# Extra products and a later place for the gates' products in the opening, silu's table loaded one phase earlier

## What is computed

```
mod = (silu(L0_c) @ L0_wmod).reshape(2, 6, 1, -1)
sa, ca, ga, sb, cb, gb = mod[:, 0], ..., mod[:, 5]
ga = (2 * (ga >= 0) - 1) * maximum(abs(ga), 0.25)
h = layernorm(x) * (1 + ca) + sa
q, k, v = h @ Wq.T, h @ Wk.T, h @ Wv.T          # rope on q and k, elu + 1
state = state + k_s v_s^T;  z = z + k_s          # over the sequence
out = (q_s @ state) / (q_s . z + 1e-6)
x = x + ga * (out @ Wo.T)
h = layernorm(x) * (1 + cb) + sb
x = x + gb * (sparsify_2to4(silu(h @ w_gate) * (h @ w_up)) @ w_down)
```

## Time and profile before

| what | value |
|---|---|
| median of 3 runs | 1020.46 us (1020.2 to 1021.85) |
| the profiled execution's own time | 1021.04 us |
| its span (first to last instruction) | 1019.1 us |
| mean granted clock of TensorE | 0.993 |
| busy: TensorE, weight loads, VectorE, ScalarE, POOL | 96%, 78%, 66%, 33%, 25% |
| opening, until TensorE's first transpose of a feature (L744) | 0 to 32.7 us |
| attention | until 538.4 us |

### The profile page before, as it was taken

One profiled execution on the slowest core, in us unless ns is written; L12 is line 12 of the kernel. 1 busy time (PEld: TensorE's weight loads), 2 busy tenths in 40 slices (PEclk: granted clock), 3 DMA queues, 4 the chain that ended last, 5 costly groups with the idle time before them and its releaser, 6 DMA issues. The chain is left out here.

```text
span 1019.1 us, 15660 instructions
## 1 busy us (share of the span) xinstructions
PE 978.2 (96%) x5978; PEld 790.9 (78%) x5978; DVE 676.8 (66%) x1488; ACT 334.1 (33%) x606; POOL 254.6 (25%) x322
## 2 busy tenths in 40 slices
PE   6899999999999999999999999998999999999997
PEld 5688888888888888888877888886666667778875
DVE  6666766667666676666666977774667776476556
ACT  4333334333344333343333331221132233322220
POOL 2222212222123231222221000024244554211111
PEclk9799999999999999999999999999999999999999
DMA  9400000000000000000004000002554440000000
GB/s 295 149 1 1 1 1 1 1 1 1 1 1 1 1 1 1 1 1 1 1 22 139 0 1 1 1 1 43 137 123 95 94 85 21 5 18 11 13 20 21
DMA packets 33051, 33.37 MB, mean 33 GB/s; under 512 B 6857, under 2 KB 26834, under 8 KB 32978
## 3 DMA queue, kind: packets, MB, share of 16 engines
q1 hardware_dynamic: 32978, 32.38, 12.0%
HBM read 23.98 MB, written 8.13 MB: 32 GB/s over the span
## 5 line engine op out<-in xcount | busy, mean ns | idle before, releaser
L411 POOL TENSOR_TENSOR rope_sum<-rope_cos,rope_sin 128x512 f32<-128x512 f32 x80 | 115.3, 1442 | 257.9 <-DVE rope_sin L544 257.9
L449 ACT ACTIVATE rope_exp<-rope_sum 128x512 f32<-128x512 f32 x80 | 50.5, 631 | 206.9 <-POOL rope_sum L411 206.7
L832 PE MATMUL proj<-wo_sb,attn_out_t 128*128 128x256 f32 x512 | 113.3, 379 | 0.7 <-issue 0.7
L832 PEld LDWEIGHTS proj<-wo_sb,attn_out_t 128*128 128x128 f32 x512 | 96.0, 190 | 13.7 <-issue 1.3
L762 PE MATMUL num<-v_ones,score_masked 128*128 128x129 f32 x512 | 99.0, 275 | 1.3 <-DVE attn_out L616 1.3
L763 PE MATMUL num<-state,q_t 128*128 128x129 f32 x512 | 99.0, 275 | 0.0
L2094 DVE SCALAR_TENSOR_TENSOR m_acc<-m_expert,gates,m_acc 128x256 f32<-128x256 f32 x128 | 61.9, 484 | 46.4 <-PE m_expert L2143 39.6
L541 DVE TENSOR_TENSOR rope_cos<-proj,cos_sb 128x512 f32<-128x512 f32 x80 | 55.3, 691 | 54.0 <-PE proj L716 54.0
L762 PEld LDWEIGHTS num<-v_ones,score_masked 128*128 128x128 f32 x512 | 82.1, 191 | 8.4 <-issue 3.1
L716 PE MATMUL proj<-w_hi,a_h_hi 128*128 128x512 f32 x192 | 79.6, 496 | 2.9 <-DVE a_h_lo L529 1.7
L763 PEld LDWEIGHTS num<-state,q_t 128*128 128x128 f32 x512 | 77.7, 192 | 0.0
(11 more groups left out here) (256 smaller groups left out, 1886.3 us busy)
## 6 DMA issues: line engine op xcount, KB each, us to landing
kv_scratch<-t_kv SPq DMA_DIRECT2D x16, 256.0 KB, 2.2
kv_rows<-kv_scratch SPq DMA_DIRECT2D x32, 128.0 KB, 3.7
a_stage<-in_wqkv SPq DMA_DIRECT2D x6, 512.0 KB, 5.3
wo_sb<-in_wo SPq DMA_DIRECT2D x1, 2048.0 KB, 9.6
a_stage<-in_wgu SPq DMA_DIRECT2D x4, 512.0 KB, 9.7
out<-x_sb SPq DMA_DIRECT2D x16, 128.0 KB, 1.7
u_scratch<-u_rows SPq DMA_DIRECT2D x28, 64.0 KB, 2.9
t_u<-u_scratch SPq DMA_DIRECT2D x14, 128.0 KB, 2.1
```

The costliest lines, as they stand in the source:

```text
L411: pool.tensor_tensor(y[:, parity], t1[:, parity], t2[:, parity], ALU.add).then_inc(s["y_done"], 1)
L832: mm = pe.matmul(proj[:, b, 0:D], o_t[:, i, :], wo[:, i, :], start=(i == 0), stop=(i == H - 1))
```

## The change

Three edits, all in the attention phase. TensorE's list now begins with a wait for `const_made` and nine products of `ident` with itself into a part of PSUM tile `num` that the gates' products overwrite later; nothing reads them. The wait for `const_made` behind the modulation vectors is gone with that. The gates' products with their wait move out of the loop over the projections to behind it. And in the last tile ScalarE applies silu to one column of `cond`, which nothing reads any more, after it rounded the last chunk.

```diff
@@ -481,6 +481,7 @@
                     if last(c, b):
                         self.chunk_high(act, NW + 3, 3 * WCH)
+                        act.activation(cond[:, 0, 0, 0:1], cond[:, 0, 0, 0:1], ACT.Silu)
                     for g in range(KVH):
@@ -694,10 +695,12 @@
             @block.tensor
             def _(pe):
+                pe.wait_ge(s["const_made"], 1)
+                for _ in range(9):
+                    pe.matmul(num[:, 0, 0:P], ident[:], ident[:], start=True, stop=True)
                 pe.wait_ge(s["silu_done"], 1)
                 pe.wait_ge(s["wmod_in"], 16)
                 pe_vectors(pe, SA, GA, True)
-                pe.wait_ge(s["const_made"], 1)
 
@@ -727,9 +730,8 @@
                         pe_vectors(pe, SB_, GB, True)
-                    if j == 4:
-                        pe.wait_ge(s["wide_done"], 1)
-                        pe_gates(pe)
+                pe.wait_ge(s["wide_done"], 1)
+                pe_gates(pe)
```

## The result

The change is slower: 1025.01 us, median of 20 runs (1021.16 to 1028.38), against 1021.44 us for the kernel before in 20 runs (1018.87 to 1028.21). The ratio is 1.0031, with a 95% interval from 1.0017 to 1.0045. The profiled execution of the change took 1024.42 us, 3.4 more than the profiled one of before. The forecast was 1019.0, 1.45 less than before, and its range ended at 1020.4; measured are 3.57 more.

The account below looks back on a forecast made before the run. TensorE's queue, busy 96% of the span, was taken as the bound, with the opening as the place to gain. Terms -1.25 - 0.3 + 0.1 + 0 = -1.45 us gave 1019.0 us against 1020.46, range 1017.5 to 1020.4.

Parts of the forecast that it names:

- what it gives arrives whole at the end of attention: Premise: time won in the first 72 us reaches attention's end undiminished, since TensorE's later waits were 0.3 us at most.
- a shift at 70 us that doesn't arrive at 1000: Sign named in advance that the forecast is wrong: time won by 70 us is missing at 1000 us; no size given.
- Part 1: Opening: nine products of ident delay the modulation's products by 0 to 0.2 us, taken as +0.1 us.
- a rival with a chance of 0.33: Opening: the warm-up raises the clock, 0.8 us more gain and the 0.1 saved; -2.4, 1018.1 us; chance 0.33.
- Part 2: Opening: gates' products behind the last projection let it start 2.4 us earlier at the lower rate, Abs 1.25 earlier; -1.25 us.
- the term of tile 0: First tile's projection: a shorter TensorE gap keeps the clock up, so the pair at 42.19 us runs faster; -0.3 us.
- The slower rival of this term: Opening: gates' products stay at the lower level and hold up Abs; +2.2, 1022.7 us; chance 0.04.
- Part 3: Last tile: silu's table load moved into ScalarE's idle time; it was hidden before, so 0 us.
- slower by over 0.2%: Whole kernel: outcome made of the gates' products becoming the bound and a little of the clock's fall; chance 0.05.
- the rival of the clock's fall in the first tile: First tile: gaps drop the clock, projection and numerators at half rate; +0.9 to +2.6 on -1.45, about 1020.2 us; chance 0.08.

Follow-up runs that it names:

- Narrow: The change with its nine products cut to two columns each, same 36 instructions; 1024.63 us, ratio 1.0026 to before.
- the writes first: SyncE issues both samples' key writes before waiting: on the change 1017.63 us, on before 1020.18, on the change without the nine products 1018.22.
- the table alone: The kernel before with only silu's table loaded early; 1021.21 us, ratio 1.0003 to before.
- wide warm-up: The change with two products of 512 columns in place of its nine of 128; 1024.0 us, ratio 1.0024 to before.
- the nine alone: The kernel before with only the nine products of ident added; 1022.89 us, ratio 1.0016 to before.
- realigned: The change with 36 instructions taken out in the scan's tile 0 by merging unread products; 1020.47 us, ratio 0.9994 to before.
- the wide fill: The change with two 512-column opening products and two unread 384-column products in the scan's tile 3; 1020.41 us, ratio 0.9983 to before.

## Why the prediction was wrong

- **The step that failed** is a premise: "what it gives arrives whole at the end of attention, because TensorE waits there for nothing that has a time of its own". As said it holds, 4.05 us arrive there. What came then is a sign that the prediction itself named, a shift at 70 us that doesn't arrive at 1000: the change is 4.07 us ahead at 70 us and 3.29 behind at 1000. The sum was taken to the end of the kernel, and the waits had been read to 500 us only. At 764 us TensorE waits for a chain of four DMA steps (write, rows, write, rows), already for 0.74 us in the profile of before: there was no slack, and each microsecond that these transfers lose is TensorE's.
- **Part 1's price** was asked in the wrong coin: 18 products by 0.22 us, +0.1 us where they stand. That term was right (5.58 against 5.53). What was left out, at nothing and without a reason, is their 36 places in TensorE's list. Narrow, with these and nothing else beside parts 2 and 3, stands 0.33% behind the change without them (ratios 1.0026 and 0.9993), 3.4 us; the two were measured on different chips, and their intervals overlap a little (from 1.0003, up to 1.0016). That the fetch moves is seen in the traces; that the late write makes the wait is shown by the runs with the queue's new order, where the fetch is in the writes and no wait follows.
- **The clock rose** with the warm-up, a rival with a chance of 0.33, but not in every execution: 2.21 us for the modulation's products in one, 3.41 in another of the same kernel. The Trainium skill, "TensorE: Matmul & The Clock Gate" (Part 1), says that the count behind a rise runs freely of the kernel's start; the two traces bear that out. The gain in the traces where it rose was more than the 0.8 us forecast: 537.42 to 534.70 makes 2.7 by the feed-forward phase. Where it didn't rise the forecast had a loss of 0.1, and the traces have a gain too, 1.1 to 1.8 (536.31 at the latest, 535.64 at the earliest): there the clock was down for 3.4 us or not at all around the last projection, and for 6.8 without the nine products. Why they do that isn't shown. Nor is it settled how the gain falls to 0.6 in the medians with the writes first.
- **Part 2:** forecast -1.55 with the term of tile 0, measured -1.33 by the trace without the warm-up, and -1.96 in the medians with the writes first. The mechanism was right almost to the row. In the trace without the nine products the last projection starts at 28.71 us at the lower level (forecast 28.67), the clock is back at 31.9 (32.4), Abs starts at 35.99 (35.87) behind the Exp and not behind the gates, and tile 0's first projection at 41.07 (40.9):

```profile
28.71 1.22 PE L717 MATMUL proj<-w_hi,a_h_hi 128*128 128x512 f32 x2 [1.35 <-DVE w_lo L148]
...
35.99 1.00 ACT L202 ACTIVATE score_masked<-num 128x1024 f32<-128x1024 f32 x1
```

  The slower rival of this term didn't happen.
- **The clock in tile 0** stayed up, also where the nine products weren't there to help. The Trainium skill, "TensorE: Matmul & The Clock Gate" (Part 4), would have let it fall where there are only transposes, which by it don't count as work. From 32.6 to 38.3 us in the change, and from 35.1 to 41.1 without the nine products, TensorE had transposes, one score product and gaps, and the windows stay at 1.00; that speaks against it here. The fall at 9.8 us in the change, behind two transposes and gaps, would agree with it.
- **Part 3:** 0 forecast, and 0 it is: the load is hidden, and the 0.29 us of the table alone stand at 45 us already, before the load.
- **The chances:** slower by over 0.2% had 0.05, all of it on the opening. No rival lay behind 70 us, though 949 us of the span do. A slip beside that: the rival of the clock's fall in the first tile, with +0.9 to +2.6 on -1.45, lies between 1019.9 and 1021.6 us, and the 1020.2 given for it is near its low end.

What stays open: which collision made 7 of the wide warm-up's 12 executions late, what makes those of before late, and what decides whether a wait brings the clock down. Length alone doesn't: every trace has a wait of 1.61 us at the scan's start, at 698 to 701 us, with no fall behind it:

```profile
698.32 1.13 PE L1781 MATMUL g_ps<-ident_n,ident 128*128 128x128 f32 x8 [1.61 <-PEq L864]
```

Nor do the 36 instructions alone say where the fetch comes: with before's list of TensorE, it stood behind 8584 products and loads in before and behind 8509 in before with the writes first. By count the 36 instructions go with late executions (36 of 55 in the four series with them and no fill, of the change, the nine alone and narrow; 10 of 37 in the three without them: the table alone, the change without the nine, realigned; and 38 of 139 of before, the same share as those three), and the queue's order decides (none of 36 with the writes first). But a trace shows one execution, and no late one of the wide kernel or of before was profiled.

## What to carry to other kernels

Instructions added at the front of a long list moved later fetches of that list here, and one landed in a DMA that had no slack: after such a change look at every wait behind it, to the end of the kernel, and at what DMA each hangs on. In a queue that issues a write, waits for it and reads it back, issue all writes that are ready before the first wait, so that one late transfer delays itself alone; here that made of the change's loss of 3.6 us a gain of 3.6. When a kernel's times are spread wide, count the late ones, of the kernel before as well: one profile, or a median, says little.

## What the runs showed of the hardware

- One 16 KB fetch of program took 1.0 to 1.7 us of one DMA engine (2.0% of 16 in 3 us in narrow, 10.1% in 1 us in the change). In tile 3 the first write of 256 KB took 2.3 to 2.6 us to its rows in the ten traces without a fetch in it, and 3.2 to 4.2 in the seven with one. The second, in the old order, took 3.5 to 3.7 without one or with one near its end, and 5.1 with one in its middle (realigned, the change without the nine, the wide fill). That the fetch is the cause is read from this agreement; no run moved the fetch alone.
- Behind seven waits of 1.4 to 2.4 us in the scan (six at 763 to 766 us, one at 839) the granted clock went from 2.4 to 1.2 GHz for 3 to 20 us: the wait of 2.24 us was followed by 10.3 us at the lower level, which cost 4.3 us. Two waits of 1.29 us at 763 us, and the wait of 1.61 us at the scan's start in every trace, were followed by no fall.
- In the change the clock, risen at about 6.4 us, fell at 9.8, after 2 us with little but two transposes, and was back at 16.6; it fell again at 23.4, behind products of two columns and a gap, and was back at 26.8. The last projection at 27.68 ran at full rate, where the forecast had it at half.
